# ScalarE's DMA queue for the row maxima alone, all stack transfers on SyncE, high and low parts a unit later in layer 1

## The chip, the cores and the metric

The kernel runs on one core of one Trainium2 chip. The metric is the device time of one execution in microseconds (us). TensorE is called PE in the profile, its weight loads PEld, VectorE DVE, ScalarE ACT, GpSimd POOL and SyncE SP.

## What is computed

Two transformer layers over x of shape (8, 256, 128) in float32. In each layer xn = layernorm(x), and x becomes x + attention(xn) + ffn(xn).

```python
# layer 0: 16 heads of 8, causal; layer 1: 16 query heads, 4 key heads, rotary
scores = einsum('bhqd,bhkd->bhqk', q, k) / sqrt(8)
weights = softmax(where(causal, scores, -inf))
out = einsum('bhqk,bhkd->bhqd', weights, v).reshape(B, T, C) @ Wo + bo
# ffn 0: top 2 of 8 experts with capacity 40, relu;  ffn 1: top 2 of 8 experts, gelu
```

## The kernel before

**A pipeline over 16 batches.** Layer and batch form a sequence n = 0 to 15 (8 of layer 0, then 8 of layer 1). `attention_plan()` (L135) writes out one list that all engines follow, each taking from it the items that are its own, in the list's order. Stage t (0 to 18) has 12 units u. In it, batch a = t gets its projections (`qk`, `val`) and its parts; batch b = t-1 gets its plain scores (`nat`) and their row maxima (`max`); batch c = t-2 gets its transposed scores (`st`), `exp`, and the products with the values (`pv`); batch d = t-3 is transposed back, normalised, projected and added. Items of the experts stand between them: in layer 0 batch e = t-4 is combined (`py`, `po`, `px`, `pl`). Stages 4 to 8 begin at 131.97, 151.45, 170.53, 190.89 and 209.74 us of the profiled execution, stages 9 to 15 at 231.32, 252.08, 273.85, 294.12, 315.68, 334.20 and 352.96; stage 3 begins at 111.52. After stage 2 all of layer 0's experts run, after stage 15 all of layer 1's (to 459 us), and then the three last stages.

**High and low parts.** The scores are products of float32 values that are split in two float32r parts. PE's `qk` fills the banks M1 (and in layer 1 M0). ScalarE's `high` (`hi`, L863) writes the high part into XQ, VectorE's `low` (`lo`, L1142) the rest. In layer 1, VectorE first applies the rotary tables (L1167) and GpSimd subtracts (`rotate`, L779), and `high` waits for that.

**Stacks.** SyncE's `stack` (L577) writes XQ to DRAM (scr) with four DMAs, waits for all, and loads it back as operands of the score matmuls: NS in layer 0 (`spread`, five DMAs, 768 KB), S1 in layer 1 (eight DMAs; S1 lies in NS too). In layer 0 ScalarE's `again` (L894) loads the same parts again, 768 KB, the other way round as TS for the transposed scores, one DMA of 384 KB and four of 96 KB, one per unit from 3 to 7.

**Maxima.** The negated row maxima NM of a batch go, half the heads at a time (h = 0 and 1), through a transpose on PE (`mxt`, L1619), into a high part (ScalarE L892) and a low part (VectorE L1190) in MS, 8 rows. SyncE's `mrow` (L613) sends MS to DRAM (leg 0, scm<-MS), waits, and loads it back as two further rows of TS or S1 (leg 1: one DMA of 16 KB in layer 0, TS<-scm; two of 8 KB in layer 1, NS<-scm). With them `st` subtracts the maxima inside the matmul. The rows of h = 0 are wanted by `st` of unit 0, those of h = 1 by `st` of unit 6. In the list `mxt` and `mrow` of h = 0 stand at unit 6 of the stage before, those of h = 1 at unit 1 of the stage itself.

**Banks.** `nat` uses N0 and N1 by turns, freed by `max` (L1140); `st` uses S0 and S1, freed by `exp` (L885). Thus unit u's `nat` waits for unit u-2's maximum, unit u's `st` for unit u-2's exp. A wait stands in an engine's queue: what comes behind it waits too.

Of the kernel before, what the change touches and what calls it, by code (L numbers as in the profile page):

```python
# [35 lines left out]
NSTK = 3  # L36
# [98 lines left out]
def attention_plan():  # L135
# [3 lines left out]
    for t in range(2 * NB + 3):  # L139
# [15 lines left out]
        for u in range(12):  # L155
            if u == 0:
                add("qk", a)
                add("hi", a)
            if a and u == a[0]:
                add("lo", a)  # L160
# [11 lines left out]
            add("exp", c, u // 3, u % 3)  # L172
            if u % 3 == 2 and t - 2 < PE_MASK:
                add("msk", c, u // 3)
# [7 lines left out]
            if u == 1:  # L182
                add("mxt", c, 1)
                add("mrow", c, 1)
                add("stack", a)
                add("ocp", d, 1)
            if u == 2:
                add("val", a)
            if 3 <= u < 8 and b and b[0] == 0:
                add("again", b, u - 3)  # L190
# [131 lines left out]
def build(nc, w, table, wp_d, moe_d, b2_d, out):  # L322
    ctx = ExitStack()
    with ctx:
# [247 lines left out]
        def _(sp):  # L572
# [31 lines left out]

            def spread(to, dense, apart, done):

                to = to[:].bitcast(F32)
                sp.dma_start(to[0:QK_ROWS, 0:KS, :], dense.rearrange("(c r d) s t -> (r d s) c t", r=4, d=HD)).then_inc(done, 16)
                for r in range(4):
                    sp.dma_start(to[24 * r:24 * r + 24, KS:, :].rearrange("x (c r) t -> x r c t", r=4)[:, r],  # L610
                                 apart.rearrange("(c r d) s t -> r (d s) c t", r=4, d=HD)[r]).then_inc(done, 16)

            def mrow(L, b, h):  # L613

                n = 2 * seq(L, b) + h
                sp.wait_ge(mlo_ok, n + 1)
                sp.dma_start(scm[L][b][h], MS[h][:].bitcast(F32)).then_inc(scm_w[h], 16)
                sp.wait_ge(scm_w[h], 16 * (seq(L, b) + 1))
                if L == 0:
                    at = KS + 8 * h  # L620
                    sp.dma_start(TS[b % 2][QK_ROWS:QK_ROWS + 2, at:at + 8, :].bitcast(F32), scm[L][b][h].rearrange("j s t -> s j t"))\
                      .then_inc(mt_in[b % 2][h], 16)
                    return
                for p in range(2):
                    r = 2 * h + p
                    sp.dma_start(S1[b % NSTK][0][QK_ROWS + 2 * r:QK_ROWS + 2 * r + 2].bitcast(F32),
                                 scm[L][b][h].rearrange("(p c) s t -> p s c t", p=2)[p])\
                      .then_inc(m1_in[b % NSTK][h], 16)

            def attention(plan):  # L630
                for item in plan:
                    if item[0] == "stack":
                        stack(*item[1:])
                    if item[0] == "mrow":
                        mrow(*item[1:])
# [190 lines left out]
        def _(act):  # L826
# [67 lines left out]
            def again(L, b, j):  # L894

                if b < 2:
                    act.wait_ge(zero_ok, 3 + b)
                else:
                    await_full(act, "S1", ("st", L, b - 2, 3, 2))
                act.wait_ge(scr_w, 64 * (b + 1))  # L900
                to = TS[b % 2][:].bitcast(F32)
                if j == 0:
                    act.dma_start(to[0:QK_ROWS, 0:KS, :], scr[L][b][1].rearrange("(c r d) s t -> (r d s) c t", r=4, d=HD))\
                       .then_inc(ts_in[b % 2], 16)
                else:
                    act.dma_start(to[24 * j - 24:24 * j, KS:, :].rearrange("x (c r) t -> x r c t", r=4)[:, j - 1],
                                  scr[L][b][0].rearrange("(c r d) s t -> r (d s) c t", r=4, d=HD)[j - 1])\
                       .then_inc(ts_in[b % 2], 16)
# [83 lines left out]
            def attention(plan):  # L992
                for item in plan:
# [14 lines left out]
                    if k == "again":  # L1008
                        again(*item[1:])
# [834 lines left out]
```

## Time and profile before

| | |
|---|---|
| time, median of 3 runs | 497.09 us (496.85 to 499.26) |
| time of the profiled execution | 498.41 us |
| its span on the core | 496.7 us |
| PE busy | 436.3 us, 88% |
| DVE busy | 321.8 us, 65% |
| ACT busy | 240.1 us, 48% |
| POOL busy | 184.9 us, 37% |
| queue of SP (q1): MB, share of 16 engines | 35.12, 25.4% |
| queue of ACT (q10) | 12.03, 8.2% |

A row of the timeline gives start and duration in us, engine, line, operation, out<-in, and in brackets how long the engine had been idle before it and what ended that. SPq and ACTq are the issues of DMAs by those engines. The profile merges neighbours of one kind (x2); their starts then lie closer than the duration says, because an engine overlaps the end of one with the begin of the next. The buffers S1 appear as NS, since they lie in it.

### The profile page before, as it was taken

To read this page: it belongs to the slowest core of one execution; us is meant where nothing else is said; L and a number is where in the kernel's file an instruction comes from. 1 tells how busy PE (TensorE), PEld (TensorE's weight loads), DVE (VectorE), ACT (ScalarE), POOL (GpSimd) and SP (SyncE) were. 2 spreads that over 40 slices of the span, in tenths; PEclk is the share of its full clock that TensorE was granted. 3 is DMA by queue.
4 is the path that set the end of the run, shared out by engine and by line. 5 is a ranking of instruction groups with operands and counts; after the bars stand their busy time and mean duration, and the time that the engine had idled before them with its cause. 6 is when DMAs were issued, how large, how long until landed. Compare 5 with 4: busy or idle time off the path is not lost.

```text
span 496.7 us, 9940 instructions
## 1 busy us (share of the span) xinstructions
PE 436.3 (88%) x3263; PEld 307.8 (62%) x3263; DVE 321.8 (65%) x988; ACT 240.1 (48%) x565; POOL 184.9 (37%) x234
## 2 busy tenths in 40 slices
PE   2568899997999899999999997999997999999985
PEld 1444446765666576665656655566557998998642
DVE  4554770117587777787877788767564666776665
ACT  2511355443655556553645435455463555555562
POOL 6570010002152543544445441666430444444100
PEclk9999999999999999999999999999997999999999
DMA  6447062323364653632236452142242122211233
GB/s 172 137 102 180 15 193 63 110 83 114 83 178 117 156 162 82 176 121 84 83 100 225 147 158 84 42 133 75 65 119 69 54 71 60 71 52 35 59 110 107
DMA packets 55216, 52.76 MB, mean 106 GB/s; under 512 B 5312, under 2 KB 50000, under 8 KB 55168
## 3 DMA queue, kind: packets, MB, share of 16 engines
q1 hardware_dynamic: 44208, 35.12, 25.4%
q10 hardware_dynamic: 8528, 12.03, 8.2%
q0 software_dynamic: 2432, 5.01, 3.4%
q8 instruction: 26, 0.43, 0.4%
q14 instruction: 22, 0.18, 0.1%
HBM read 33.09 MB, written 19.04 MB: 105 GB/s over the span
## 4 chain that ended last, share of the span: by engine, by line
PE 58%; DMA 12%; DVE 12%; issue 6%; SPq 4%; ACT 4%; POOL 3%; DVEq 0%; ACTq 0%; POOLq 0%
PE ps_P L1611 6%; PE ps_N L1743 5%; DMA scm<-MS 5%; DMA scr<-XQ 4%; PE ps_N L1544 4%; PE ps_M L1784 3%; PE ps_M L1753 3%; PE ps_P L1753 3%; PE ps_S L1743 3%; PE ps_M L1654 3%; PE ps_S L1589 3%; PE ps_N L1555 2%; PE ps_N L1550 2%; DVE NM L1140 2%; PE ps_S L1575 2%
## 5 line engine op out<-in xcount | busy, mean ns | idle before, releaser
L885 ACT ACTIVATE PT<-ps_S 128x512 f32<-128x512 f32 x192 | 112.3, 591 | 80.5 <-PE ps_S L1589 39.3
L1140 DVE TENSOR_REDUCE NM<-ps_N 128x2 f32<-128x512 f32 (+1 forms) x192 | 127.2, 680 | 35.5 <-PE ps_N L1550 22.7
L737 POOL TENSOR_SCALAR_AFFINE_SELECT PT<-PT 128x512 f32<-128x512 f32 x80 | 49.0, 636 | 139.2 <-ACT PT L885 139.2
L1544 PE MATMUL ps_N<-maskb,identb 128*128 128x256 bf16 (+1 forms) x192 | 62.0, 323 | 2.6 <-DVE NM L1140 1.7
L803 POOL DMA_INDIRECT yt<-LATE,EI x39 | 38.9, 997 | 56.3 <-DVE LATE L1378 46.6
L1611 PE MATMUL ps_P<-PT,VA 128*16 128x256 f32 (+1 forms) x1024 | 54.0, 328 | 0.4 <-ACT PT L885 0.4
L1550 PE MATMUL ps_N<-NS 96*128 96x512 f32 x96 | 52.8, 554 | 0.0
L1555 PE MATMUL ps_N<-NS 96*128 96x256 f32 (+1 forms) x128 | 49.4, 427 | 0.0
L1589 PE MATMUL ps_S<-NS 100*128 100x512 f32 (+1 forms) x96 | 46.2, 485 | 1.6 <-ACT PT L885 1.6
L1611 PEld LDWEIGHTS ps_P<-PT,VA 128*16 128x16 f32 x1024 | 23.3, 96 | 34.3 <-issue 20.5
L987 ACT ACTIVATE LATE<-ps_N,ucol 128x128 f32<-128x128 f32 x104 | 29.8, 369 | 27.4 <-PE ps_N L1743 26.0
L1575 PE MATMUL ps_S<-TS 98*128 98x512 f32 x96 | 39.0, 406 | 2.9 <-ACT PT L885 1.6
L795 POOL DMA_INDIRECT xs<-XI,slot x32 | 31.0, 968 | 20.9 <-DVE slot L1328 10.0
L1544 PEld LDWEIGHTS ps_N<-maskb,identb 128*128 128x128 bf16 x192 | 19.9, 103 | 21.8 <-issue 10.2
L1743 PE MATMUL ps_N<-LATE 128*128 128x128 f32 x208 | 30.3, 291 | 2.0 <-issue 0.8
L1743 PEld LDWEIGHTS ps_N<-LATE 128*128 128x128 f32 x208 | 26.9, 202 | 4.4 <-DVE LATE L1355 3.6
L1363 DVE COPY LATE<-EW 128x512 f32 x39 | 18.5, 473 | 13.5 <-PE ps_M L1753 9.0
L1586 PE MATMUL ps_S<-identb,maskb 128*128 128x256 bf16 (+1 forms) x72 | 22.9, 318 | 3.4 <-ACT PT L885 2.2
L1415 DVE TENSOR_SCALAR LATE<-ps_M,consts 128x320 f32 x8 | 4.4, 551 | 33.0 <-PE ps_M L1784 33.0
L1555 PEld LDWEIGHTS ps_N<-NS 96*128 96x128 f32 x128 | 24.8, 194 | 1.4
L1355 DVE COPY LATE<-EW 128x512 f32 x39 | 16.8, 430 | 9.4 <-PE ps_N L1743 4.4
L1575 PEld LDWEIGHTS ps_S<-TS 98*128 98x128 f32 x96 | 18.7, 194 | 5.6 <-issue 2.6
(197 smaller groups left out, 845.1 us busy)
## 6 DMA issues: line engine op xcount, KB each, us to landing
scr<-XQ SPq DMA_DIRECT2D x24, 256.0 KB
NS<-scr SPq DMA_DIRECT2D x64, 96.0 KB
ROT<-in_L_ffn_W SPq DMA_DIRECT2D x16, 256.0 KB, 3.1
EW<-in_moe ACTq DMA_DIRECT2D x8, 512.0 KB, 3.8
scr<-XQ SPq DMA_DIRECT2D x24, 128.0 KB
NS<-scr SPq DMA_DIRECT2D x8, 384.0 KB
TS<-scr ACTq DMA_DIRECT2D x8, 384.0 KB
TS<-scr ACTq DMA_DIRECT2D x32, 96.0 KB
```

Source lines behind the costliest of these rows:

```text
L737: last = pool.affine_select(out=v, in_=v, compare_op=ALU.is_ge, fill=0.0, base=0, pattern=[[0, 4], [1, P]], channel_multiplier=-1)
L795: pool.indirect_dma_start(xs, bass.IndirectOffsetOnAxis(ap=slot[:, i, k:k + 1], axis=0), XI[:, i, :], None)\
L803: pool.indirect_dma_start(yt, bass.IndirectOffsetOnAxis(ap=EI[:, j // GRP % 3, j % GRP:j % GRP + 1], axis=0), E_Y[j % 4], None).then_inc(y ...
L885: act.activation(PT[:, n % NPT, r, :], bank[s][:], ACT.Exp, scale=SCALE).then_inc(exp_ok, 1)
L1140: dve.tensor_reduce(to, x, AX.X, ALU.max, negate=True).then_inc(nm_ok, 1)
L1544: mm(diag, identb[:], maskb[:, None, :].broadcast_to((P, many, P)), start=True, stop=False, skip_group_check=True)
L1550: mm(s[:], NS[b % 2][0:QK_ROWS, c, q], NS[b % 2][0:QK_ROWS, at:at + many, 0:w_], start=False, stop=True, skip_group_check=True).then_inc(f ...
L1555: last = mm(s[:, 2 * w_ * i:2 * w_ * (i + 1)], sq[0:QK_ROWS, c, q], sk[0:QK_ROWS, r:r + 2, 0:w_], start=False, stop=True, skip_group_check ...
L1575: mm(s[:], TS[b % 2][0:QK_ROWS + 2, g, k], TS[b % 2][0:QK_ROWS + 2, at:at + many, T - n:T], start=True, stop=True).then_inc(full[f"S{u % 2 ...
L1589: mm(s[:], sk[rows, g, k], sq[rows, c:c + many, T - n:T], start=not masked, stop=True, skip_group_check=masked).then_inc(full[f"S{u % 2}"], 1)
L1611: last = mm(o, va[:, kt, head, :], pr, start=(kt == 0), stop=(kt == 1))
L1743: last = mm(o[:, P * m:P * (m + 1)], E_W1[j % 2][:, P * m:P * (m + 1)], E_XT[j % 2], start=True, stop=True)
```

## The change

- `hi` and `lo` of layer 0 stay in unit 0, but `lo` comes after the unit's first `max` instead of ahead of its `nat`. In layer 1 `hi` moves from unit 0 to unit 1 behind `exp`, `lo` from unit 1 to unit 2 behind `max` and `exp`.
- `again` becomes one item at unit 0, on SyncE, with all its five DMAs (through `spread`), ahead of `stack`, which moves from unit 1 to unit 0.
- `mrow` is gone from SyncE. ScalarE's `max_out` (`mout`) issues leg 0 at unit 2 and leg 1 at unit 4 for h = 1, and leg 0 at unit 7 and leg 1 at unit 9 for h = 0, each behind the unit's `exp`. Leg 0 waits for the low maxima, leg 1 for leg 0's landing, now in ScalarE's queue.
- The loads of layer 1's expert weights (`ew`, 512 KB each, stages 10 and 11, units 0, 3, 6 and 9) stay on ScalarE.

```diff
         for u in range(12):
             if u == 0:
                 add("qk", a)
-                add("hi", a)
-            if a and u == a[0]:
-                add("lo", a)
+                if t < NB:
+                    add("hi", a)
...
             add("max", b, u)
             add("exp", c, u // 3, u % 3)
+            if u == 0 and t < NB:
+                add("lo", a)
+            if u == 1 and t >= NB:
+                add("hi", a)
+            if u == 2 and t >= NB:
+                add("lo", a)
...
             if u == 1:
                 add("mxt", c, 1)
                 add("mrow", c, 1)
-                add("stack", a)
                 add("ocp", d, 1)
             if u == 2:
                 add("val", a)
-            if 3 <= u < 8 and b and b[0] == 0:
-                add("again", b, u - 3)
+            if u == 0:
+                if b and b[0] == 0:
+                    add("again", b)
+                add("stack", a)
+            if u in (2, 4):
+                add("mout", c, 1, (u - 2) // 2)
+            if u in (7, 9):
+                add("mout", b, 0, (u - 7) // 2)
...
+            def again(L, b):
+
+                if b < 2:
+                    sp.wait_ge(zero_ok, 3 + b)
+                else:
+                    await_full(sp, "S1", ("st", L, b - 2, 3, 2))
+                spread(TS[b % 2], scr[L][b][1], scr[L][b][0], ts_in[b % 2])
...
+            def max_out(L, b, h, leg):
+
+                n = 2 * seq(L, b) + h
+                if leg == 0:
+                    act.wait_ge(mlo_ok, n + 1)
+                    act.dma_start(scm[L][b][h], MS[h][:].bitcast(F32)).then_inc(scm_w[h], 16)
+                    return
+                act.wait_ge(scm_w[h], 16 * (seq(L, b) + 1))
+                if L == 0:
+                    at = KS + 8 * h
+                    act.dma_start(TS[b % 2][QK_ROWS:QK_ROWS + 2, at:at + 8, :].bitcast(F32), scm[L][b][h].rearrange("j s t -> s j t"))\
+                       .then_inc(mt_in[b % 2][h], 16)
+                    return
+                for p in range(2):
+                    r = 2 * h + p
+                    act.dma_start(S1[b % NSTK][0][QK_ROWS + 2 * r:QK_ROWS + 2 * r + 2].bitcast(F32),
+                                  scm[L][b][h].rearrange("(p c) s t -> p s c t", p=2)[p])\
+                       .then_inc(m1_in[b % NSTK][h], 16)
```

## Rows read from the trace of the kernel before

**Rows 1.** The page, part 4: the chain that ended last, shares by line.
```profile
PE ps_P L1611 6%; PE ps_N L1743 5%; DMA scm<-MS 5%; DMA scr<-XQ 4%; PE ps_N L1544 4%; PE ps_M L1784 3%; PE ps_M L1753 3%; PE ps_P L1753 3%; PE ps_S L1743 3%; PE ps_M L1654 3%; PE ps_S L1589 3%; PE ps_N L1555 2%; PE ps_N L1550 2%; DVE NM L1140 2%; PE ps_S L1575 2%
```

**Rows 2.** Busy time in windows, TensorE, summed over stages 3 to 14.
```profile
sum 241.44, PE 221.85; mean PE 18.49
```

**Rows 3.** Who waited for whom, TensorE: us in total, times, longest us.
```profile
PE ps_S L1575 <- DMA TS<-scm: 1.3, 2, 0.9
PE ps_S L1586 <- DMA NS<-scm: 1.0, 2, 0.7
```

**Rows 4.** Chain in order of time (start, us), stage 5; last, VectorE's timeline.
```profile
156.82 1.44 DMA scm<-MS
...
159.98 3.94 DMA scr<-XQ
...
166.04 4.87 DMA scm<-MS
...
170.93 1.91 DMA TS<-scm
...
163.47 0.41 DVE L1190 TENSOR_TENSOR MS<-ps_M,MS 8x256 fp32r<-8x256 f32 x1
```

**Rows 5.** Timeline of TensorE, start of stage 6: `nat` and `st` of unit 0.
```profile
171.53 0.59 PE L1550 MATMUL ps_N<-NS 96*128 96x512 f32 x1
172.98 0.48 PE L1575 MATMUL ps_S<-TS 98*128 98x512 f32 x1 [0.86 <-DMA TS<-scm]
```

**Rows 6.** Timelines of stage 4, units 0 to 6: VectorE, ScalarE, TensorE.
```profile
134.07 0.88 DVE L1148 SCALAR_TENSOR_TENSOR XQ<-ps_M,consts,XQ 128x256 fp32r<-128x256 f32 x2 [2.31 <-ACT XQ L871]
136.28 0.41 DVE L1190 TENSOR_TENSOR MS<-ps_M,MS 8x256 fp32r<-8x256 f32 x1
...
138.86 0.60 ACT L885 ACTIVATE PT<-ps_S 128x512 f32<-128x512 f32 x1 [0.79 <-PE ps_S L1575]
139.35 0.53 ACT L951 ACTIVATE LATE<-ps_M 120x256 f32<-120x256 f32 x2
...
135.60 0.10 PEld L1544 LDWEIGHTS ps_N<-maskb,identb 128*128 128x128 bf16 x1 [0.31 <-DVE NM L1140]
...
140.03 1.57 PE L1691 MATMUL ps_M<-LATE 120*128 120x128 f32 x12
...
141.47 0.58 PE L1550 MATMUL ps_N<-NS 96*128 96x512 f32 x1
141.89 0.41 PE L1575 MATMUL ps_S<-TS 98*128 98x512 f32 x1
```

**Rows 7.** Timelines of stage 11, units 0 to 5: TensorE, ScalarE, VectorE.
```profile
279.70 0.50 PE L1589 MATMUL ps_S<-NS 100*128 100x512 f32 x1 [0.82 <-ACT PT L885]
...
284.02 1.58 PE L1691 MATMUL ps_M<-LATE 120*128 120x128 f32 x12
...
278.45 0.42 ACT L875 ACTIVATE XQ<-ROT 128x256 fp32r<-128x256 f32 x1 [4.67 <-POOL ROT L779]
...
279.08 1.05 ACT L885 ACTIVATE PT<-ps_S 128x512 f32<-128x512 f32 x2
280.03 0.36 ACT L892 ACTIVATE MS<-ps_M 8x256 fp32r<-8x256 f32 x1
...
279.20 0.75 DVE L1154 TENSOR_TENSOR XQ<-ROT,XQ 128x256 fp32r<-128x256 f32 x2 [1.74 <-ACT XQ L876]
...
280.81 1.27 DVE L1140 TENSOR_REDUCE NM<-ps_N 128x2 f32<-128x512 f32 x2
```

**Rows 8.** Timeline of SyncE's issues in stage 10; last, the page's part 6.
```profile
259.14 0.27 SPq L617 DMA_DIRECT2D scm<-MS  x1
262.24 0.53 SPq L626 DMA_DIRECT2D NS<-scm  x2
...
EW<-in_moe ACTq DMA_DIRECT2D x8, 512.0 KB, 3.8
```

**Rows 9.** Timeline of TensorE in stage 14: unit 6's `st`.
```profile
345.17 0.27 PE L1586 MATMUL ps_S<-identb,maskb 128*128 128x256 bf16 x1 [0.25 <-DMA NS<-scm]
```

More of the change, by code:

```diff
@@ L611, in spread @@
                                  apart.rearrange("(c r d) s t -> r (d s) c t", r=4, d=HD)[r]).then_inc(done, 16)
[L613 to L628, printed above, removed]
             def attention(plan):
@@ L633, in attention @@
                         stack(*item[1:])
-                    if item[0] == "mrow":
-                        mrow(*item[1:])
+                    if item[0] == "again":
+                        again(*item[1:])
                     if item[0] == "xz":
@@ L892, in max_high @@
                 act.activation(MS[h][:, 0, :], bank["M1"][0:NH // 2, 0:T], ACT.Copy).then_inc(mhi_ok, 1)
[L894 to L908, printed above, removed]
+            def max_out(L, b, h, leg):
[15 more added lines that the diff above has]
+                       .then_inc(m1_in[b % NSTK][h], 16)
             def copy_o(L, b, h):
@@ L1007, in attention @@
                         max_high(*item[1:])
-                    if k == "again":
-                        again(*item[1:])
+                    if k == "mout":
+                        max_out(*item[1:])
                     if k == "ocp":
```

## The prediction

> **What bounds the kernel now.** I read the chain that ended last first. It names DMA transfers of the maxima (scm<-MS, 5% of the span) and of the high and low parts (scr<-XQ, 4%) among its largest pieces [rows 1], which suggests that freeing them pays. The second view contradicts this: busy time in twelve consecutive stages (t = 3 to 14) sums to 241.4 us, of which TensorE is busy 221.9 [rows 2]. Only 19.6 us are idle, 1.6 per stage, so no edit of queues can bring more than a part of 19.6. The third view says who owns the idle time: TensorE waited for a maxima transfer 1.3 us in two places (L1575) and 1.0 in two (L1586) [rows 3]. All else is small waits for ScalarE and VectorE. TensorE bounds the kernel; the question is which short waits at unit boundaries go and which come.
>
> **Maxima of the first half of the heads (h = 0).** In stage 5 VectorE had them ready at 163.47 + 0.41 = 163.9, but SyncE stood in `stack` and issued scm<-MS at 166.04, behind the five loads of NS. It took 4.87 us and the second leg 1.91 more; alone the first leg took 1.44 [rows 4]. So TensorE's first st of stage 6 started 1.45 us after the matmul ahead of it and had idled 0.86 [rows 5]. Now leg 0 can leave at 163.9 and leg 1 three units on; even at 4.87 for the one and 1.91 for the other they are there at 170.7, before 171.95, where the st would stand without a wait (171.53 + 0.42, the step from 141.47 to 141.89 [rows 6]). Gain: the 1.3 us of [rows 3] (bounds 1.0 and 1.6). The later stage starts already had their rows in time and gain nothing. The transfers of `stack` start about 3 us earlier, with slack that nobody uses: priced at 0.
>
> **Layer 0, `lo` behind the first maximum.** VectorE waited 2.31 us for the high part before `lo`, and only then read the first maxima; TensorE's unit 2 waited 0.31 for that [rows 6]. Now the maximum comes first: 0.2 us less in each of stages 3 to 7 (bounds 0 and 0.3).
>
> **Layer 0, second half of the maxima (h = 1), the new risk.** ScalarE issues leg 0 when the low maxima are done, 136.28 + 0.41 = 136.7 in stage 4, as SyncE did. Leg 1 stands after exp of unit 4 (138.86) and before the eviction L951 (139.35). That eviction of two copies (0.53) releases the products at 140.03, for which TensorE already waits about 0.2 [rows 6]. A wait inside leg 1 blocks the ScalarE instructions behind it: the eviction, the next exp, and TensorE through both. With the 0.2 of the paragraph before, exp of unit 4 is at 138.7; and for the eviction to start no later than today's 139.35, with some 0.25 for leg 1's own issue, leg 0 must have landed by 139.1: 2.4 us after its issue. Alone it takes 1.44 [rows 4]. But `again` (768 KB) now leaves at the stage's start, and the scr writes, which took 3.94 us after their last issue when loads ran beside them [rows 4], begin at about 135.1 rather than after the maxima. They are in flight just then. The nearest row of a small copy beside another queue's large load: issued 259.14, the next leg 262.24, so 3.1 us [rows 8]. I take 2.5: nearest to that row, as other queues' large transfers are in flight here too, and below it because a part of them is smaller. Then the 0.2 gained is lost, plus about 0.1 per stage: -0.1 in each of four stages with that eviction (4 to 7), +0.2 in stage 3. The second leg (1.91) then lands 136.7 + 2.5 + 1.9 = 141.1, before the st of unit 6 at 141.89 [rows 6]. The bounds per stage are +0.2 and -0.7. ScalarE loses five issues per stage beside exps, which no one waited for: 0. SyncE's five `again` issues come before `stack`, whose data isn't there yet: 0.
>
> The Trainium skill speaks against this part of the change. "DMA: Bandwidth & Descriptors", section "Issuing engines are not separate DMA queues", says that transfers from any issuing engine run on the same 16 DMA engines and interleave, so a queue of its own is no lane of its own; the 3.1 us of [rows 8] agrees, the loads and the copy being on different queues. The same page, section "Queues, rings and completion order", lets each DMA engine switch between queues at packets, by which a small copy would wait for a packet or so and stay near 1.44; by that the sum would be about 1 us better.
>
> **Layer 1, `hi` and `lo` later.** ScalarE stood idle 4.67 us for rotated rows with exp of unit 0 behind it; TensorE's unit 2 then idled 0.82 [rows 7]. That goes, in eight stages: 6.6 us if nothing else were late. But follow what is next. ScalarE does exp 1 (0.5), then the two high parts (279.08 - 278.45 = 0.63), so the high maxima start at about 279.5, not 280.03. VectorE needs them for its low maxima, queued ahead of its maximum of unit 2; then comes `lo` (0.75) [rows 7], which stood before all of them while VectorE was waiting anyway. VectorE's maximum of unit 3 and the normalisation behind it therefore come about 0.1 to 0.2 us later than now. The transposes of the normalised rows (unit 5) wait for that; TensorE arrives 0.8 earlier and stands. What survives is that the products at 284.02, which wait for ScalarE's eviction, come about 0.25 earlier. So +0.25 in each of stages 8 to 11: +1.0 (bounds 0 and 3.3). In stage 12 VectorE also carries routing: -0.2.
>
> **Layer 1, the maxima.** In stages 13 to 15 there is no such product; TensorE's unit 6 already waited 0.25 for the maxima's landing [rows 9]. Leg 0 leaves 0.4 earlier, but leg 1 now goes out after exp 4 with the scr writes of the same stage started 0.5 before it instead of after it. That adds 0.5 to 1 us to 1.9. I take -0.35 each, -1.05 together (bounds +0.3 and -0.8 each). In stages 10 and 11 ScalarE's queue isn't free for the maxima: eight loads of 512 KB, 3.8 us each [rows 8], go out on it at units 0, 3, 6 and 9, so leg 1 of unit 4 stands right behind one. 3.8 from unit 3's exp plus some tenths is as late as unit 6's need: -0.4 each, -0.8 (bounds 0 and -1.5). Of the tail, where TensorE waited 0.7 in one place for this chain [rows 3]: leg 0 as now, leg 1 after an exp: -0.1.
>
> **Sum.** 1.3 + 0.2 - 0.4 + 1.0 - 0.2 - 1.05 - 0.8 - 0.1 = -0.05: no change. The profiled execution's span of 496.7 stays 496.7 or so; with 1.7 us around it that execution took 498.4, a little above the median of 497.09. Against the median I predict 497.1.
>
> **Rivals.** (1) Faster: VectorE has more room in layer 1 than I give it, and small copies stay under 2.4 us. Then half to all of the 6.6 comes back, with 0.2 in five stages and the 1.3, less 0.8 in stages 10 and 11: 4.8 to 8.1 us, the lower end likelier: 491.5. For it: 4.67 us of ScalarE's idle time is real and large. Against it: VectorE's next steps are back to back from 279.2 to 282 [rows 7]. (2) Slower: leg 1's wait blocks ScalarE whenever stacks are in flight. Each leg 0 at 3.1 us or more costs 0.7 in four layer-0 stages, 0.8 in three of layer 1, 1.5 in the two with EW: 2.8 + 2.4 + 3.0 = 8.2 against gains of 2.5 (1.3, 1.0 and 0.2), so +5.7: 502.8; it decides from 2.4 us for leg 0. For it: [rows 8]; against it: the copy has eight packets only, and could slip in. (3) The queue gives no shelter and the h = 0 maxima stay late: the 1.3 doesn't come, 498.4; unlikely, since they now leave 3 us earlier.
>
> The skill's page named above, same section on completion order, says that the increment that tells of a landing waits for every earlier write of that DMA engine, also those of other queues; by that rule the copy's landing would be told only behind part of the scr writes, as in rival 2, and the time would be rival 2's.
>
> **How the numbers follow.** Forecast 0.42 (own range 495.0 to 499.4), faster 0.30, slower 0.24, (3) 0.04. A measurement of this kernel tells 0.5%, 2.5 us, from no change. Faster by over that 0.30, within it 0.43, slower 0.27. The range 491.0 to 502.0 leaves out the outer part of both rivals, about 0.1 at each end.
>
> **What would show it.** Right: the 0.8 us waits of unit 2 for exp in layer 1 gone; in their place waits at unit 5 for ON or at unit 6 for the maxima; scm<-MS of h = 1 at 2 to 3 us; `again`, scr and NS in flight earlier; stage 6 starting its st without a gap. Wrong: layer-1 stages shorter by 0.6 us or more (rival 1); ScalarE idle before L951 with scm<-MS as releaser (rival 2); stages 10 and 11 longer than now by over 1 us.

## The result and the profile after

The changed kernel takes 508.77 us in the median of five executions (501.35 to 509.84), the kernel before 497.09 beside it (494.08 to 499.26). The two longest of the five, 509.67 (the profiled one) and 509.84, count as slow runs, and without them the changed kernel takes 1.014 times as long, 95% interval 1.0098 to 1.0185, which is 7 us more. The forecast was no change, 497.1 with a range up to 502.0. It was wrong, on the slow side and outside the range: 497.09 x 1.0141 is 504.1.

The profiled execution spans 507.9 us against 496.7, so it shows more than those 7 us, and each stage time below is that of one execution. Where a loss matters, the traces of the experiments are therefore looked at as well. Cut at the starts of the stages (the first q/k projection of each on TensorE), and ahead of the three last stages where ScalarE loads its table for the first exp behind the experts, the 11.2 us of difference lie like this:

| stretch | before, us | after, us | difference |
|---|---|---|---|
| start to stage 3 | 111.52 | 112.38 | +0.9 |
| stages 3 to 9 | 140.56 | 138.69 | -1.9 |
| stages 10, 11 | 42.04 | 46.51 | +4.5 |
| stage 12 | 21.56 | 23.43 | +1.9 |
| stages 13, 14 | 37.28 | 38.99 | +1.7 |
| stage 15 and the experts of layer 1 | 107.55 | 102.96 | -4.6 |
| the three last stages | 36.19 | 44.94 | +8.8 |

So the part for which the prediction had the most working, stages 3 to 9, went as forecast. What was lost lies in three other places: stages 10 and 11, stages 13 and 14, and the three last stages. The page's part 2, the granted clock in 40 slices (tenths of full speed):

```profile
PEclk9955999999999999999997998999999999999797
```

The two 5s at 25 to 51 us are no part of the loss, though the page of before shows a 9 there: the score matmul `nat` (96x512) takes 0.99 us in both kernels at that point (33.70 us after, 34.67 before) and 0.59 at full clock.

Its part 4, the chain that ended last, shares by line:

```profile
PE ps_P L1615 8%; PE ps_N L1548 5%; PE ps_N L1747 5%; DMA scm<-MS 4%; PE ps_M L1788 3%; PE ps_N L1554 3%; PE ps_M L1757 3%; PE ps_P L1757 3%; PE ps_S L1593 3%; PE ps_S L1579 3%; PE ps_N L1559 3%; DMA NS<-scm 3%; PE ps_S L1747 3%; PE ps_M L1695 2%; PE ps_M L1658 2%
```

Against [rows 1] scr<-XQ is gone from the list, as meant. NS<-scm, the second leg of the layer-1 maxima, has come in with 3%. The view of who waited for whom (TensorE of the changed kernel: us in total, times, longest us) says what it cost:

```profile
PE ps_S L1590 <- DMA NS<-scm: 8.2, 6, 4.5
...
PE ps_M L1669 <- ACT XT L961: 3.1, 4, 1.6
...
PE ps_P L1641 <- DVE ON L1206: 2.7, 7, 0.8
...
PE ps_S L1579 <- DMA TS<-scm: 2.1, 1, 2.1
PE ps_P L1632 <- ACT OT L920: 2.1, 6, 0.7
PE ps_M L1695 <- ACT LATE L955: 1.7, 4, 0.6
```

L1590 is the line that was L1586 and stood at 1.0 us in two places [rows 3]. Now it is 8.2 us in six, one of them 4.5. The 2.1 us for TS<-scm are one wait in stage 2, for the rows of h = 1; stage 2 with the experts behind it is 1.9 us longer, of which earlier stages give 1.0 back.

**Where 4.5 us of stages 10 and 11 went.** ScalarE's timeline, stage 10 of the changed kernel (start, us, engine, instruction, [idle before, releaser]):

```profile
263.85 0.36 ACTq L980 DMA_DIRECT2D EW<-in_moe  x1
...
270.17 0.58 ACTq L910 DMA_DIRECT2D NS<-scm  x2
270.80 0.38 ACT L961 ACTIVATE XT<-ps_M 128x256 f32<-128x256 f32 x1 [2.06 <-DMA scm<-MS]
```

The chain in order of time, the first leg of h = 0:

```profile
265.43 4.72 DMA scm<-MS
```

The maxima of the first half of the heads leave 1.6 us behind a 512 KB load of the experts' weights on the same queue, with SyncE's stack loads (NS<-scr, issued 264.10 to 267.23) in flight too. They take 4.72 us and land at 270.15; the load of the weights had landed at 267.32, the last stack load did at 271.05. In the kernel before this leg was nearly as slow (issued 270.28, the second leg at 274.17), but there it was SyncE that waited. Now the second leg stands at unit 9 in front of the copy XT<-ps_M, so ScalarE stands still 2.06 us and does that copy late. TensorE waits for it, and then something follows that is dearer than the wait. TensorE's timeline there:

```profile
271.23 0.62 PE L1669 MATMUL ps_M<-consts,LATE 128*80 128x128 f32 x2 [1.63 <-ACT XT L961]
271.65 0.42 PE L1548 MATMUL ps_N<-maskb,identb 128*128 128x256 bf16 x1
```

Busy time in windows, there and in the tail (columns: window, length, busy us and instructions of PE, PEld, DVE, ACT, POOL, then granted clock, DMA share, GB/s):

```profile
271.30:278.10 6.80, 6.80 (x33) 4.09 (x34) 2.69 (x12) 2.06 (x4) 1.23 (x2) 0.50 0.20 61
472.70:479.50 6.80, 5.55 (x25) 3.60 (x29) 2.03 (x4) 2.11 (x5) 0.00 (x0) 0.50 0.03 6
```

From 271.3 on the granted clock is 0.50 for 6.8 us: the lower of the two levels, 1.2 GHz instead of 2.4. The mask matmul L1548 takes 0.42 us here and 0.27 at full clock. TensorE is busy 6.80 of these 6.80 us and does less.

**Where 8.8 us of the three last stages went.** Windows of these stages, before and after:

```profile
460.51:496.70 36.19, 28.18 (x263) 16.30 (x255) 21.84 (x62) 18.68 (x36) 0.88 (x1) 0.97 0.32 94
```

```profile
462.96:507.90 44.94, 32.52 (x263) 18.51 (x255) 21.93 (x62) 18.95 (x36) 0.89 (x1) 0.84 0.25 76
```

SyncE's and TensorE's timelines in the first attention stage behind the experts:

```profile
465.25 2.01 SPq L661 DMA_DIRECT2D LATE<-yt  x4
...
473.95 0.37 PE L1590 MATMUL ps_S<-identb,maskb 128*128 128x256 bf16 x1 [4.46 <-DMA NS<-scm]
```

The chain in order of time, there (start, us):

```profile
466.06 3.40 DMA scm<-MS
469.74 4.07 DMA NS<-scm
```

The four loads of the experts' answers (Y<-yt, 512 KB each; the trace calls the tile LATE) leave in one burst of 2.01 us. In the kernel before, an `mrow` stood on SyncE ahead of the first, the second and the third of them, and they left at 465.74, 471.34 and (two) 480.05. Now nothing holds SyncE, and both legs of the maxima, 16 KB each, travel beside 2 MB. TensorE waits 4.46 us for the second leg, and the other window at clock 0.50 above begins 1.3 us before this wait ends.

**What was won ahead of it: 4.6 us.** Who waited for whom, TensorE, before and after:

```profile
PE ps_M L1733 <- DMA LATE<-xs: 3.3, 1, 3.3
```

```profile
PE ps_M L1737 <- DMA LATE<-xs: 0.6, 1, 0.6
```

LATE<-xs is the first load of layer 1's experts. On SyncE it stood behind the `mrow` of stage 15 and left 18.8 us into the stage; now it leaves at 17.0. The profile of before also has 6.8 us at the lower clock right behind that wait of 3.3 us (375.16 to 381.99), the changed kernel has none there.

Both differences recur. Five profiled executions have the changed queues and no such hold of SyncE as e5 and e8 add (this one and those of e1 to e4 below): 102.7 to 103.1 us from stage 15 to the last stages and 42.9 to 45.2 for these. Five have the old queues (before, e6, e7, e9, e10): 105.9 to 107.6 and 36.2 to 37.8.

**Stages 13 and 14.** SyncE's, ScalarE's and TensorE's timelines in stage 13:

```profile
328.97 0.38 SPq L593 DMA_DIRECT2D scr<-XQ  x1
...
329.61 0.55 ACTq L910 DMA_DIRECT2D NS<-scm  x2
...
332.77 0.27 PE L1590 MATMUL ps_S<-identb,maskb 128*128 128x256 bf16 x1 [0.84 <-DMA NS<-scm]
```

The second leg leaves 0.64 us behind the first write of the stack to scr instead of ahead of it, and the st of unit 6 waits 0.84 us for it.

### The profile page after: what moved, and what is told of

It reads as the page before. It is cut to its first block, busy times and chain, and to the rows that moved or that the text cites. A ratio compares the mean times of both kernels' runs of the same rounds, so it can differ in the third digit from the quotient of the medians.

```text
span 507.9 us, 9900 instructions
## 1 busy us (share of the span) xinstructions
PE 439.7 (87%) x3263; PEld 305.0 (60%) x3263; DVE 324.2 (64%) x988; ACT 241.2 (47%) x565; POOL 188.6 (37%) x234
## 4 chain that ended last, share of the span: by engine, by line
PE 68%; DMA 11%; DVE 9%; ACT 5%; issue 5%; ACTq 1%; POOL 0%; DVEq 0%; SPq 0%
PE ps_P L1615 8%; PE ps_N L1548 5%; PE ps_N L1747 5%; DMA scm<-MS 4%; PE ps_M L1788 3%; PE ps_N L1554 3%; PE ps_M L1757 3%; PE ps_P L1757 3%; PE ps_S L1593 3%; PE ps_S L1579 3%; PE ps_N L1559 3%; DMA NS<-scm 3%; PE ps_S L1747 3%; PE ps_M L1695 2%; PE ps_M L1658 2%
## 5 line engine op out<-in xcount | busy, mean ns | idle before, releaser
L1144 DVE TENSOR_REDUCE NM<-ps_N 128x2 f32<-128x512 f32 (+1 forms) x192 | 128.5, 682 | 51.5 <-PE ps_N L1554 29.6
L738 POOL TENSOR_SCALAR_AFFINE_SELECT PT<-PT 128x512 f32<-128x512 f32 x80 | 51.3, 665 | 138.1 <-ACT PT L886 138.1
L1548 PE MATMUL ps_N<-maskb,identb 128*128 128x256 bf16 (+1 forms) x192 | 63.0, 328 | 1.8 <-DVE NM L1144 0.7
L1615 PE MATMUL ps_P<-PT,VA 128*16 128x256 f32 (+1 forms) x1024 | 55.9, 338 | 0.4 <-ACT PT L886 0.4
L1559 PE MATMUL ps_N<-NS 96*128 96x256 f32 (+1 forms) x128 | 51.4, 443 | 0.0
L1593 PE MATMUL ps_S<-NS 100*128 100x512 f32 (+1 forms) x96 | 48.3, 507 | 0.0
L796 POOL DMA_INDIRECT xs<-XI,slot x32 | 32.4, 1013 | 22.1 <-ACT PT L886 16.9
L1548 PEld LDWEIGHTS ps_N<-maskb,identb 128*128 128x128 bf16 x192 | 20.8, 108 | 20.9 <-issue 9.7
L1194 DVE TENSOR_TENSOR MS<-ps_M,MS 8x256 fp32r<-8x256 f32 x32 | 13.2, 412 | 28.8 <-ACT MS L893 28.2
L1590 PE MATMUL ps_S<-identb,maskb 128*128 128x256 bf16 (+1 forms) x72 | 23.7, 329 | 8.2 <-DMA NS<-scm 8.2
L1747 PE MATMUL ps_N<-LATE 128*128 128x128 f32 x208 | 28.5, 280 | 1.9 <-issue 0.9
L1747 PEld LDWEIGHTS ps_N<-LATE 128*128 128x128 f32 x208 | 25.2, 191 | 4.4 <-DVE LATE L1359 3.3
L1559 PEld LDWEIGHTS ps_N<-NS 96*128 96x128 f32 x128 | 26.0, 203 | 1.7
```

Source lines behind the costliest of these rows:

```text
L738: last = pool.affine_select(out=v, in_=v, compare_op=ALU.is_ge, fill=0.0, base=0, pattern=[[0, 4], [1, P]], channel_multiplier=-1)
L796: pool.indirect_dma_start(xs, bass.IndirectOffsetOnAxis(ap=slot[:, i, k:k + 1], axis=0), XI[:, i, :], None)\
L1144: dve.tensor_reduce(to, x, AX.X, ALU.max, negate=True).then_inc(nm_ok, 1)
L1548: mm(diag, identb[:], maskb[:, None, :].broadcast_to((P, many, P)), start=True, stop=False, skip_group_check=True)
L1559: last = mm(s[:, 2 * w_ * i:2 * w_ * (i + 1)], sq[0:QK_ROWS, c, q], sk[0:QK_ROWS, r:r + 2, 0:w_], start=False, stop=True, skip_group_check ...
L1593: mm(s[:], sk[rows, g, k], sq[rows, c:c + many, T - n:T], start=not masked, stop=True, skip_group_check=masked).then_inc(full[f"S{u % 2}"], 1)
```

## The experiments

Eleven runs of nine kernels, in three groups. The kernel before had medians of 498.3, 498.87 and 498.96 us beside them; ratios are to that.

**e1: the answers held, all but the first.**

```diff
+                    if item[0] == "mout" and item[4] == 1 and seq(*item[1:3]) >= 14:
+                        sp.wait_ge(scm_w[item[3]], 16 * (seq(*item[1:3]) + 1))
                     if item[0] == "ans":
                         answers(item[1])
```

> The changed kernel, but from the maxima of sequence 14 on SyncE also waits for the landing of each first leg (scm<-MS) before it goes on, so that the four loads Y<-yt again leave one by one, as in the kernel before. Nothing of the maxima's own path moves. Theory A (the tail's loss is the answers): NS<-scm behind the experts lands some 3 us earlier, TensorE's idle 4.46 us at L1590 falls to under 1, the half clock behind it goes, stage 15 to the end is 143.7 us again instead of 147.9, and the whole is 4 to 5 us shorter than the changed kernel: 503 to 504 us. Theory B (the maxima on ScalarE's queue are late by themselves, the answers only happen to be there): the first st of the tail still waits 3 us or more, and the time stays at 507 to 509 us.

Measured: 507.34 us (506.24 to 512.11), ratio 1.0157, 95% 1.0104 to 1.0209: theory B's time. But the edit held less than it should have. SyncE's timeline in the tail:

```profile
467.48 11.25 SPq L663 DMA_DIRECT2D LATE<-yt  x3
```

The chain in order of time:

```profile
468.29 2.86 DMA scm<-MS
471.45 2.96 DMA NS<-scm
```

The first answer stands at unit 3, ahead of the hold at unit 4, and so still left 0.8 us ahead of the first leg; the second left at 471.16 with the second leg. One answer in flight beside each leg gives 2.86 and 2.96 us, four gave 3.40 and 4.07. The run tells nothing on the tail's cause yet; it gives the middle point of a series.

**e2: the experts' weights on SyncE's queue.**

```diff
-                    if k == "ew":
-                        expert_weights(item[1])
...
+                    if item[0] == "ew":
+                        sp.wait_ge(exp_ok, 96 + 3 * item[1] + 1)
+                        expert_weights(item[1])
```

> The changed kernel, but the nine loads of the experts' weights and biases (EW, B2) leave on SyncE's queue, each behind the same exp as now. Theory A (the loss of stages 10 and 11 is the EW load that is ahead of scm<-MS on one queue): scm<-MS of unit 7 in stage 10 takes 2 to 3 us instead of 4.72, TensorE's idle 1.63 us before L1669 goes and with it the half clock of 6.8 us; stage 10 is 3 us shorter, stage 11 1 us: 504 to 505 us. Theory B (all queues share the same engines, so which queue a large load stands on says nothing): scm<-MS takes 4 us or more still, stages 10 and 11 stay as long: 508 us.

Measured: 503.59 us, ratio 1.0106, 95% 1.0041 to 1.017. Theory A's time. ScalarE's and TensorE's timelines of stage 10:

```profile
271.44 0.54 ACTq L920 DMA_DIRECT2D NS<-scm  x2
272.13 0.38 ACT L971 ACTIVATE XT<-ps_M 128x256 f32<-128x256 f32 x1 [0.91 <-PE ps_M L1705]
...
263.96 1.58 PE L1696 MATMUL ps_M<-LATE 120*128 120x128 f32 x12 [1.01 <-ACT LATE L965]
```

The chain in order of time, the first leg of h = 1:

```profile
259.45 3.16 DMA scm<-MS
```

The window of stage 10:

```profile
252.99:275.36 22.37, 19.73 (x165) 12.79 (x162) 16.95 (x53) 10.96 (x24) 10.57 (x16) 1.00 0.57 178
```

The copy into XT is released by TensorE's own products again, the clock stays at 1.00, and the two stages take 42.2 us against 46.5 (42.0 in the kernel before). Yet scm<-MS of h = 0 was issued at 267.90 and its second leg could leave at 271.44, 3.5 us later, not the 2 to 3 expected. And the other leg, h = 1, took 3.16 us and cost 1.01 us at the eviction, a wait that in no other stage was so long. The edit moved the loads in time, too: they queued behind the stack's, and two of them left together at 267.59, 0.3 us ahead of this leg. So the run doesn't show what the queue is worth by itself. It shows that the leg is slow beside large loads of the other queue alone (3.5 us), and that nothing is lost at XT<-ps_M when the wait ends before TensorE's products for it are there.

**e3: the second leg of h = 0 behind the copies of unit 9.**

```diff
-            if u in (7, 9):
-                add("mout", b, 0, (u - 7) // 2)
+            if u == 7:
+                add("mout", b, 0, 0)
...
             if u == 9:
                 add("pv", c, 1)
                 layer1("px", e)
                 ffn0("gt", g, 1)
                 ffn0("gte", g, 1)
+            if u == 9:
+                add("mout", b, 0, 1)
```

> The changed kernel, but the second leg of the first half's maxima (h = 0) stands behind the copies of unit 9 (ScalarE's XT<-ps_M and GT<-ps_M) instead of in front of them. Theory A (it is the wait inside the queue of ScalarE that costs, not the transfer): the second leg leaves just as late, but no one needs it before the next stage, so TensorE's idle before L1669 (3.1 us in 4 places) goes, with the half clock behind it in stage 10: 3 to 4 us shorter, 504 to 505 us. Theory B (the transfer itself is too late for the next stage, too): the idle moves to the st of unit 0 of the next stages, and the time stays at 508 us.

Measured: 503.8 us, ratio 1.0103, 95% 1.0065 to 1.0141. Theory A. ScalarE's timeline in stage 10:

```profile
264.60 0.28 ACTq L902 DMA_DIRECT2D scm<-MS  x1
...
268.82 0.38 ACT L963 ACTIVATE XT<-ps_M 128x256 f32<-128x256 f32 x1 [0.90 <-PE ps_M L1706]
...
269.71 0.54 ACTq L912 DMA_DIRECT2D NS<-scm  x2
```

The window of stage 10:

```profile
250.18:272.05 21.87, 19.73 (x165) 12.78 (x162) 16.93 (x53) 11.00 (x24) 10.56 (x16) 1.00 0.63 184
```

Here the EW load is still ahead on the same queue, and the first leg is still slow: it took 4.14 us. Nobody needs its rows so soon. Only the place of the *wait* was moved, by some instructions, and 4.5 us are back: 42.0 us for stages 10 and 11, what they took before the change. This rests on the stages: the three profiled executions without the wait in front of that copy or without its lateness (e2, e3, e5) have 41.9 to 42.2 us there, the two with it (the changed kernel, e1) 46.5 and 45.7. The whole times of e3 and of the changed kernel, with ratios of 1.0103 and 1.014, have intervals that overlap.

**e4: high and low parts back at their old places.**

```diff
             if u == 0:
                 add("qk", a)
-                if t < NB:
-                    add("hi", a)
+                add("hi", a)
+            if a and u == a[0]:
+                add("lo", a)
...
-            if u == 0 and t < NB:
-                add("lo", a)
-            if u == 1 and t >= NB:
-                add("hi", a)
-            if u == 2 and t >= NB:
-                add("lo", a)
```

> The changed kernel with the high and low parts back at the places of the kernel before, in both layers; only the queues differ from the kernel before. Theory A (the later parts gain a little in layer 1's quiet stages and cost nothing): the waits for exp of unit 2 come back, stages 8 and 9 are 0.4 us longer each, stages 12 to 15 unchanged in their excess: 508 to 511 us. Theory B (the later parts put scr writes beside the maxima of h = 1 and VectorE's work behind time, and are the cause of the loss in stages 10 to 15): these stages lose their excess of 8 us, NS<-scm of h = 1 falls from 2.4 to 3.4 us to under 2: 500 to 502 us.

Measured: 518.79 us (514.85 to 519.77), ratio 1.0377, 95% 1.0308 to 1.0446. Theory B is refuted, and theory A's amount is too small by far. The new queues alone cost 19 to 20 us (by the ratio and by the medians), and the later parts give 10 to 12 of that back. With the high part early, the writes to scr leave at 261.19 to 262.69 us, in stage 10, just around scm<-MS (262.13). This first leg of h = 1 lands only at 266.38, and ScalarE's eviction stands behind the wait for it. TensorE's timeline:

```profile
267.77 1.58 PE L1690 MATMUL ps_M<-LATE 120*128 120x128 f32 x12 [2.61 <-ACT LATE L950]
```

Of the 19.9 us by which its span (516.6) is longer than that of the kernel before, 9.2 lie in stages 10 and 11, 3.7 in 13 and 14 and 2.5 from stage 15 on. That its small copies are slower because more large ones run beside them is argued from these times, not tested.

**e5: e3 with the answers really held.**

```diff
+                    if item[0] == "mrow" and seq(*item[1:3]) >= 14:
+                        sp.wait_ge(m1_in[item[2] % NSTK][item[3]], 32 * (item[2] // NSTK + 1))
                     if item[0] == "ans":
                         answers(item[1])
```

> As e3_behind_px (second leg of h = 0 behind the copies of unit 9), and in the tail SyncE waits at the place of the old mrow for the landing of NS<-scm, so that no answer (Y<-yt) is in flight beside either leg of sequences 14 and 15; in e1 the first answer had still left before the first leg, since it stands at unit 3 and the hold stood at unit 4. Theory A (the tail's loss is answers in flight beside small copies): scm<-MS takes 1.5 and NS<-scm 1.9 us there, the idle before the st of unit 6 falls from 4.84 to under 0.5, stage 15 to the end is 143 to 144.5 us instead of 147.7, the whole 499.5 to 501. Theory B (the place on ScalarE's queue costs by itself): idle of 2 us or more stays, 503 to 504 us.

Measured: 501.21 us (496.67 to 505.63), ratio 1.0019, 95% 0.9977 to 1.0062: level with the kernel before. ScalarE's and TensorE's timelines in the tail:

```profile
467.73 0.54 ACTq L914 DMA_DIRECT2D NS<-scm  x2
...
469.82 0.27 PE L1594 MATMUL ps_S<-identb,maskb 128*128 128x256 bf16 x1 [0.56 <-DMA NS<-scm]
```

The chain in order of time:

```profile
467.99 1.70 DMA NS<-scm
```

With nothing in flight beside it the second leg takes 1.70 us, TensorE's wait is 0.56 instead of 4.46, the three last stages take 37.3 us against 44.9 in e3, and stage 15 to the end takes 141.6 us (500.0 - 358.42) against 147.7, even under the 143 to 144.5 expected. Theory A. It is under the 143.7 of the kernel before because the experts' part stays short (104.3 us), though the edit also holds SyncE in stage 15 and TensorE's wait for LATE<-xs there is 2.0 us. Part of the 0.56 that is left is the queue's own: the first leg had landed at 467.30, and the second left at 467.73, when its turn on ScalarE had come.

**e6: the later high and low parts alone**, in the kernel before:

```diff
-                add("hi", a)
-            if a and u == a[0]:
-                add("lo", a)
+                if t < NB:
+                    add("hi", a)
...
+            if u == 0 and t < NB:
+                add("lo", a)
+            if u == 1 and t >= NB:
+                add("hi", a)
+            if u == 2 and t >= NB:
+                add("lo", a)
```

> The kernel before with the later high and low parts alone (both layers); queues as in the kernel before. Theory A (that part is the gain that e4 shows from the other side, 10 us there because it also shelters the maxima on ScalarE's queue; alone it is worth the 0.45 us of stages 8 and 9 and as much in 10 to 14): 3 to 4 us faster than the kernel before, ratio 0.992 to 0.994. Theory B (it is worth the full 10 us of e4): ratio 0.98. Theory C (the maxima on SyncE then stand in front of a stack that is ready later, and the next stage's nat waits for NS<-scr): no gain, ratio 1.0 or above, with TensorE waits on NS<-scr in stages 11 to 15.

Measured: 495.5 us, ratio 0.9939, 95% 0.9908 to 0.997. Theory A. Stages 8 to 11 are shorter than before by 0.44, 0.47, 0.62 and 0.45 us.

**e7 and e9: a pause of TensorE by itself.** In the kernel before, once, in stage 10 (e9: 2 in place of 4):

```diff
                 await_full(act, f"M{b % 2}", ("px", 1, b))
+                for _ in range(4 if b == 6 else 0):
+                    act.activation(XT[:, T * b:T * (b + 1)], bank[f"M{b % 2}"][:, 0:T], ACT.Copy).then_inc(idle_ok, 1)
+                    act.wait_ge(idle_ok, _ + 1)
```

> The kernel before with one pause put in: in stage 10 ScalarE makes four more copies, one waiting for the other, ahead of XT<-ps_M, so that TensorE's next instruction on XT comes some 1.5 to 2 us later, once. Theory A (a pause of TensorE of that length is followed by a stretch at half the granted clock, as in the changed kernel at 271.3): a stretch at clock 0.5 of 3.4 or 6.8 us begins within 2 us of the pause, and the stage is 1.5 us for the pause and 2 to 3 us for the clock longer: the whole +4 us, 502 us. Theory B (the half clock in the changed kernel came by chance, or from elsewhere): no such stretch there, the stage longer by the pause alone: 500 us.

> As e7_idle, with two further copies instead of four, so that the pause is about half (0.7 to 0.9 us over the usual). Theory A (any pause near a microsecond brings the half clock): a stretch at 0.5 follows it again and stage 10 is 2.5 us or more longer than the 21.8 us of before. Theory B (a short pause passes without it, as TensorE's waits of 0.8 to 1.0 us for exp do in the kernel before): stage 10 about 22.6 us, no stretch at 0.5 there, the time within 1 us of the kernel before plus 0.8.

Measured: e7 503.8 us, ratio 1.0102 (1.0075 to 1.0129); e9 502.19 us, ratio 1.0047 (1.0013 to 1.0082). TensorE's timeline at the pause in e7:

```profile
270.67 0.65 PE L1669 MATMUL ps_M<-consts,LATE 128*80 128x128 f32 x2 [2.13 <-ACT XT L961]
```

Windows of e7, 6.8 us from 0.7 us before the end of the pause, and stage 10:

```profile
270.00:276.80 6.80, 6.13 (x32) 4.05 (x32) 2.70 (x12) 2.64 (x6) 1.22 (x2) 0.51 0.22 71
250.08:275.46 25.38, 21.72 (x165) 14.42 (x161) 17.77 (x56) 12.36 (x28) 10.66 (x18) 0.89 0.50 159
```

TensorE's timeline at the pause in e9:

```profile
270.66 0.41 PE L1669 MATMUL ps_M<-consts,LATE 128*80 128x128 f32 x2 [1.30 <-ACT XT L961]
```

Windows of e9, stage 10, and 3.4 us behind the pause:

```profile
250.83:274.04 23.21, 20.36 (x165) 13.30 (x161) 17.39 (x56) 11.59 (x26) 10.61 (x18) 0.97 0.52 159
272.80:276.20 3.40, 3.40 (x21) 1.72 (x15) 1.48 (x8) 0.58 (x1) 1.22 (x2) 0.50 0.34 102
```

The usual idle time here is 0.47 us. In e7 1.66 were added, and stages 10 and 11 are 4.2 us longer than in the kernel before (25.38 + 20.88 against 21.77 + 20.27): the pause and some 2.5 more, with 6.8 us at the lower clock. In e9 0.83 were added, and both stages together are 2.4 longer: the pause and 1.6 more, with 3.4 us at the lower clock, which began 2.1 us after the end of the pause. Theory A in both. The Trainium skill, "TensorE: Matmul & The Clock Gate", section "Part 1: The HAM clock gate", says that TensorE's clock is gated by how busy it has recently been. The clock of 0.51 and 0.50 in these rows agrees.

**e8, e10, e11: h = 1 back on SyncE.** The changed kernel with `mrow` of h = 1 as in the kernel before, e3's place for the second leg of h = 0, and the hold in the tail:

```diff
             if u == 1:
                 add("mxt", c, 1)
                 add("mrow", c, 1)
+                add("stack", a)
...
                 if b and b[0] == 0:
                     add("again", b)
-                add("stack", a)
-            if u in (2, 4):
-                add("mout", c, 1, (u - 2) // 2)
...
+                    if item[0] == "mrow" and item[3] == 1:
+                        mrow(*item[1:])
+                    if item[0] == "mrow" and item[3] == 0 and seq(*item[1:3]) >= 14:
+                        sp.wait_ge(m1_in[item[2] % NSTK][0], 32 * (item[2] // NSTK + 1))
```

> The changed kernel with the second half's maxima (h = 1) back on SyncE, both legs at unit 1 ahead of the stack, as in the kernel before; the first half's (h = 0) on ScalarE's queue, the second leg behind unit 9's copies; in the tail SyncE waits for the landing of sequence 15's h = 0 maxima before the next answer. Theory A (SyncE's order kept scr<-XQ behind NS<-scm, and that is what stages 13 to 15 and the eviction waits of stages 4 to 7 lost): NS<-scm of h = 1 takes under 2.1 us again, the 0.9 us waits of stages 12 to 15 and 0.6 us of stages 4 to 7 go, the tail is 143.7 us: 494 to 496 us, faster than the kernel before by 0.5 to 1 per cent. Theory B (again on SyncE and the queue of h = 0 cost by themselves): 498 us or more.

> e6_hilo_only once more in more rounds, to stand beside e8 on one chip. Theory A (the first half's maxima and `again` in their new places are worth something by themselves): e8's kernel is shorter than this one by 1 to 1.5 us, ratios to before 0.994 and 0.991. Theory B (they are worth nothing): both ratios the same within 0.001.

> e8_mixed once more in more rounds: by theory A ratio 0.989 to 0.992 and 1 to 1.5 us shorter than e10_hilo_again; by theory B the same as e10_hilo_again.

Measured: e8 494.17 us, ratio 0.9903 (0.9872 to 0.9933); again as e11 494.01, ratio 0.9908 (0.9875 to 0.994), beside e10 with 496.42, ratio 0.9952 (0.9923 to 0.9982). So this kernel beats both others: 0.9% shorter than the kernel before and, with 2.4 us between the medians (1.3 between those of e8 and e6), shorter than the later parts alone, though the intervals of the two ratios overlap. SyncE's and TensorE's timelines in stage 13 of e8:

```profile
319.18 0.55 SPq L636 DMA_DIRECT2D NS<-scm  x2
319.77 0.38 SPq L593 DMA_DIRECT2D scr<-XQ  x1
...
321.40 0.27 PE L1611 MATMUL ps_S<-identb,maskb 128*128 128x256 bf16 x1 [0.21 <-DMA NS<-scm]
```

The chain in order of time:

```profile
319.45 1.82 DMA NS<-scm
```

The order on one queue keeps scr<-XQ behind NS<-scm, which takes 1.82 us again (2.76 in the changed kernel) and costs TensorE 0.21 instead of 0.84. What the moved h = 0 adds over e10 shows in who waited for whom, one line of e10 and then nothing of its kind in e11:

```profile
PE ps_S L1580 <- DMA TS<-scm: 2.0, 2, 1.5
```

That is the wait of [rows 3], which comes and goes with the slow first leg behind the loads of NS in SyncE's queue (1.3 us in the profile before, 2.0 in e10). The hold of SyncE in e8 stands in stage 15, too: TensorE's wait for LATE<-xs is 3.1 us there, as with the old queues, so the 4.6 us of the experts' part are not won in this kernel.

## Why the prediction was wrong

**Right: what bounds, and the first two terms.** h = 0 in layer 0: +1.3 was forecast; stages 5 and 6 are 0.45 and 1.10 shorter, and their waits for TS<-scm (0.41 and 0.86) are gone. h = 1 in layer 0: the first leg was taken at 2.5 us with the threshold at 2.4, to cost a little at the eviction. ScalarE and TensorE in stage 5 of the changed kernel:

```profile
157.68 0.28 ACTq L900 DMA_DIRECT2D scm<-MS  x1
159.94 0.23 ACTq L905 DMA_DIRECT2D TS<-scm  x1
...
160.96 1.24 PE L1695 MATMUL ps_M<-LATE 120*128 120x128 f32 x9 [0.26 <-ACT LATE L955]
```

The second leg could leave 2.26 us behind the first. Stages 3 to 7 together are 0.97 us shorter; the terms gave 1.1. Singly they fit less well: stages 3 and 4, for which the terms gave 0.2 less and 0.1 more, are 0.18 and 0.43 longer, with a wait of 0.62 for the eviction in stage 4. In e8, where h = 1 leaves ScalarE's queue, stage 5's wait for this eviction is gone.

**Right mechanism, size off: the high and low parts.** The 0.82 us waits for exp [rows 7] went, and waits for ON and OT came in their place (2.7 and 2.1 us in the list above, 1.1 and 0.9 before), much as the step said. It let 0.25 per stage survive; stages 8 and 9 gained 0.44 and 0.46, and e6 confirms it with 0.44 to 0.62 in four stages. The term +1.0 should have been +2.0. That it is worth 10 to 12 us beside the new queues (e4) was not seen at all.

**Right mechanism, size off: h = 1 in stages 13 and 14.** The step named the scr writes that now run beside the second leg and took -0.35 per stage, bound -0.8. It was 1.0 and 0.7, the first outside the bound. The leg took about what was allowed (the chain has 2.76 us from its second part on), but the step counted the 0.4 us that the first leg leaves earlier as kept. ScalarE issues the second leg only behind exp 4: 329.61 - 321.01 = 8.6 us into the stage, and SyncE had issued it 8.5 us into it. Nothing of the 0.4 was left.

**Wrong: "leg 1 of unit 4 stands right behind one", -0.4 in each of stages 10 and 11.** The queue was seen, the wrong victim was named. Of h = 1 nothing much came. (In e4, with the high parts early, h = 1 did cost: 2.61 us at the eviction.) The cost came from h = 0: its leg 0, slow beside the EW load and the stack loads as it had been before, and leg 1's wait for it, now in front of XT<-ps_M. The prediction asked who stands behind the waiting instruction only for the wait at unit 4, never for the one at unit 9, because the rows of h = 0 are not needed before the next stage. The rows had the slack, the wait had not: it stands in ScalarE's program between two copies that TensorE needs at once. e3 shows it: the rows are late there, too, the wait stands elsewhere, and 4.5 us are back. The term was -4.5 instead of -0.8.

**Wrong, and the largest miss: the tail, -0.1.** It was -8.8 in the three last stages. The step priced the legs and forgot what `mrow` had done for others. It was SyncE's wait in `mrow` that held the answers back. Each queue that a step leaves was to be asked for what then runs free, and SyncE's four answers were not in the sum. The same question would have found the gain: the experts' first load, also held by `mrow`, now leaves 1.8 us earlier, and TensorE waits 2.7 us less for it. Together with the lower clock that the profile of before has behind that wait this is +4.6 which the sum had not. That the whole is not longer still is, as to this part, luck. In flight beside a leg of 16 KB, measured:

| beside it | first leg, us | second leg, us | run |
|---|---|---|---|
| nothing | 1.44 [rows 4] | 1.70 | e5 |
| one answer of 512 KB | 2.86 | 2.96 | e1 |
| four answers in a burst | 3.40 | 4.07 | changed kernel |

The prediction set the rule of the Trainium skill ("DMA: Bandwidth & Descriptors", section "Queues, rings and completion order") that the engines go from queue to queue at packets against the rule that an increment lands behind every earlier write of its engine. The first alone would leave a small copy near 1.44 us whatever is in flight, and the table (2.86 to 4.07) speaks against that. It fits the second, or both together; no run here parts them further.

**Not in the sum: what a pause does to TensorE's clock.** In stage 10 and in the tail, the idle time that the change added, 1.2 us (1.63 less the usual 0.47) and 4.5, came with 6.8 us at the lower level each, right behind the wait in stage 10, from 1.3 us before its end in the tail. e7 and e9 put 1.6 to 2.5 us on it. The waits of under 1 us in the profile of before had no such stretch behind them; those of 2.95 us (stage 3) and 3.29 us (LATE<-xs) had. Of the 4.5 us of stages 10 and 11 about half is this, if the 2.5 of e7 holds for the shorter wait there.

**The range.** It ended at 502.0, below the 502.8 at which the prediction's own slower rival stood with a chance of 0.24. That rival had ScalarE blocked by leg 1's wait, which is what happened in stages 10 and 11, but counted 0.7 in each of four layer-0 stages, which together came out near the forecast, and nothing for the tail.

**Open.** Stage 12's 1.9 us. It has a wait of 0.55 for NS<-scm, but also a stretch of 3.4 us at the lower clock behind TensorE's long wait for the row maxima. In e2 and e3, where this stage's maxima and parts stand as in the changed kernel and which lack this stretch, the stage takes 21.8 us, 0.3 more than before. The stretch comes and goes with the same code. The window of stage 12 in e8, and in e11:

```profile
288.44:310.27 21.83, 18.36 (x168) 11.59 (x164) 19.75 (x58) 9.45 (x20) 8.13 (x10) 1.00 0.23 68
```

```profile
287.06:310.50 23.44, 19.98 (x168) 12.77 (x164) 19.88 (x58) 9.45 (x20) 8.57 (x10) 0.93 0.24 72
```

The same kernel takes 21.83 us there in one execution and 23.44 in the other. Part of the difference between the two profiled executions is therefore chance, and so is part of the spread of the changed kernel's times (501.35 to 509.84). Open, too, is which transfers e4's small copies wait for.

## What to carry to other kernels

When a wait moves to another engine, ask two things of it: what stands behind the wait in its new place, down to each copy that the bounding engine needs (even where the data has much slack), and what its old place was holding back. An order on one queue is a schedule; splitting it over two lets large transfers run beside the small ones that were ahead of them, and here a 16 KB copy that had taken 1.44 to 1.9 us then took 2 to 4.1. It can also free what stood behind a wait for nothing: the experts' first load left 1.8 us earlier. And a new pause of a nearly saturated TensorE may cost itself and another 1.6 to 2.5 us of lower clock; here one of 1.3 us did.

## What the hardware showed that was not expected

- One pause of 1.30 us was followed, 2.1 us later, by 3.4 us at half clock, and 6.8 us at half clock began 0.8 us before the end of one of 2.13 us. By the ratios the whole kernel became 2.3 and 5.1 us longer (0.47% and 1.02%, e9 and e7; 95% intervals 0.13 to 0.82% and 0.75 to 1.29%) for 0.83 and 1.66 us of added idle time. It doesn't follow each time: the wait in stage 12, 2.3 us, was followed by it in e11 and not in e8.
- In the tail of the changed kernel the answers landed at 469.30, 470.75, 472.26 and 473.69, and the small copy, issued 0.4 us behind the second of them, at 466.06 + 3.40 = 469.46. It neither slipped by nor waited for all that had been issued ahead of it on the other queue.
